# Routed down products: both weight parts in one 512-column matmul, and the two halves added on VectorE

## The reference

```python
out = x @ W_base.T + b_base                       # _L0_cond_ref
lora = einsum('bter,eor,be->bto', einsum('btc,erc->bter', x, As), Bs, w)
h = out + lora * 2.0
scores = softmax(h @ gate_w.T); topk_w, topk_i = top_k(scores, 2)
combine = zeros((T, 8)).at[arange(T)[:, None], topk_i].set(topk_w / topk_w.sum(-1) * 2.5)
g = silu(einsum('td,edf->etf', h, w_gate)) * einsum('td,edf->etf', h, w_up)
y = einsum('te,etd->td', combine, einsum('etf,efd->etd', g, w_down))
return x + y + silu(h @ sw_gate) * (h @ sw_up) @ sw_down
```

## Time and profile before

| | |
|---|---|
| median of 3 runs | 530.56 us (528.44 to 532.13) |
| the profiled execution | 530.44 us |
| its span, first to last instruction | 528.7 us |
| mean granted clock of TensorE | 0.997 of 2.4 GHz |
| busy: PE, DVE, ACT, POOL | 95%, 59%, 52%, 47% of the span |

### The profile page before, as it was taken

One profiled execution on the slowest core, in us unless ns is written; L12 is line 12 of the kernel. 1 busy time (PEld: TensorE's weight loads), 2 busy tenths in 40 slices (PEclk: granted clock), 3 DMA queues, 4 the chain that ended last, 5 costly groups with the idle time before them and its releaser, 6 DMA issues.

```text
span 528.7 us, 10655 instructions
## 1 busy us (share of the span) xinstructions
PE 500.3 (95%) x3284; PEld 461.4 (87%) x3285; DVE 311.4 (59%) x693; ACT 276.3 (52%) x596; POOL 249.4 (47%) x367
## 2 busy tenths in 40 slices
PE   8999998899999999988899999999998999999997
PEld 7988987788888889978899898988988999888886
DVE  2676757998987454434555444444444434368986
ACT  3567776456662445556455455555554645444422
POOL 2142427454650635655876666656666763310100
PEclk9999999999999999999999999999999998999999
DMA  7387479056122253633344334333433442399952
GB/s 221 134 266 202 161 201 323 5 184 180 42 81 40 91 138 91 109 102 91 101 118 110 109 102 117 104 105 100 109 110 100 120 113 66 82 366 311 377 179 79
DMA packets 104923, 74.56 MB, mean 141 GB/s; under 512 B 61930, under 2 KB 99828, under 8 KB 104884
## 3 DMA queue, kind: packets, MB, share of 16 engines
q1 hardware_dynamic: 95764, 55.21, 36.0%
q0 software_dynamic: 6816, 18.62, 11.8%
q10 hardware_dynamic: 2304, 0.26, 0.5%
HBM read 40.25 MB, written 20.32 MB: 115 GB/s over the span
## 4 chain that ended last, share of the span: by engine, by line
PE 57%; DVE 14%; issue 9%; ACT 7%; DMA 5%; SPq 2%; another core or an unknown queue 2%; POOL 1%; DVEq 0%; ACTq 0%; POOLq 0%
PE bank L273 17%; PE bank L275 16%; PE bank L274 16%; PE bank L751 5%; DMA turned<-rows 2%; SPq L342 2%; DVE bank L1213 2%; ACT gt_h L933 1%; ACT x_half L857 1%; DVE acc L1306 1%; DVE xt_l L1028 1%; DMA rows<-x_halves,tok_i 1%; DVE gt_l L1284 1%; PE bank L569 1%
## 5 line engine op out<-in xcount | busy, mean ns | idle before, releaser
L273 PE MATMUL bank<-w_hi,rt_h 128*128 x284 | 98.2, 346 | 0.0
L274 PE MATMUL bank<-w_lo,rt_h 128*128 x284 | 91.9, 324 | 0.0
L275 PE MATMUL bank<-w_hi,rt_l 128*128 x284 | 91.8, 323 | 0.0
L1284 DVE TENSOR_TENSOR gt_l<-bank,gt_h 128x384 fp32r<-128x384 f32 x71 | 39.6, 558 | 84.0 <-ACT gt_h L949 73.5
L544 POOL DMA_INDIRECT y_rows<-y_sb,dst_i x71 | 71.9, 1012 | 11.2 <-POOL spare L458 10.0
L537 POOL DMA_INDIRECT rows<-x_halves,tok_i x71 | 69.5, 979 | 12.5 <-issue 2.2
L933 ACT CAST gt_h<-bank 128x512 fp32r<-128x512 f32 (+1 forms) x48 | 28.1, 586 | 89.3 <-DVE bank L1213 80.5
L273 PE MATMUL bank<-xs_h,sg_h 128*128 128x512 f32 x176 | 70.7, 402 | 0.6 <-ACT act L923 0.4
L273 PE MATMUL bank<-w_hi,gt_h 128*128 (+1 forms) x213 | 61.9, 290 | 9.6 <-DVE gt_l L1284 9.5
L274 PE MATMUL bank<-xs_l,sg_h 128*128 128x512 f32 x176 | 68.9, 391 | 0.0
L275 PE MATMUL bank<-xs_h,sg_l 128*128 128x512 f32 x176 | 68.7, 390 | 0.0
(11 more groups left out here) (181 smaller groups left out, 1228.4 us busy)
## 6 DMA issues: line engine op xcount, KB each, us to landing
pick<-y_rows SPq DMA_DIRECT2D x16, 512.0 KB, 7.9
xin<-in_x_dram SPq DMA_DIRECT2D x8, 512.0 KB, 4.7
x_halves<-x_half SPq DMA_DIRECT2D x8, 512.0 KB, 3.3
w_own<-in_L_ffn_w_gate_dram SPq DMA_DIRECT2D x8, 352.0 KB, 4.3
w_own<-in_L_ffn_w_up_dram SPq DMA_DIRECT2D x8, 352.0 KB, 4.7
y_sb<-in_x_dram SPq DMA_DIRECT2D x5, 512.0 KB, 3.7
base_rows<-y_sb SPq DMA_DIRECT2D x5, 512.0 KB, 2.8
acc<-base_rows SPq DMA_DIRECT2D x5, 512.0 KB, 7.3
```

The source lines that it names most:

```text
L273: pe.matmul(o, lh, rh, start=start, stop=False, skip_group_check=skip)
L274: pe.matmul(o, lh, rl, start=False, stop=False, skip_group_check=skip)
L275: return pe.matmul(o, ll, rh, start=False, stop=stop, skip_group_check=skip)
L1284: v.tensor_tensor(gt_l[i % 2][:, 0:FC * P], TB[:, 0:FC * P], gt_h[i % 2][:, 0:FC * P].bitcast(F32), ALU.subtract).then_inc(s_gl, 1)
```

## The change

The high and the low parts of the routed weights, two tensors before, become the two halves of one tensor, `w_all`. That alone moves nothing, but it lets one matmul read both parts. In `e_down` the first two of the three passes, which had the same stationary operand `gt_h`, become one matmul with 2 x 256 moving columns; it writes high by high into the first half of the bank and high by low into the second half. The third pass stays and adds to the first half. The result of a block is now the sum of the two halves of its bank, and so the copy on ACT is replaced by a `tensor_reduce` with add on DVE, over pairs that lie 256 columns apart. It stands in DVE's loop after `r_word_low` and ahead of `e_low`.

```diff
-        w_hi = sb("w_hi", [P, E, REC], F32R)
-        w_lo = sb("w_lo", [P, E, REC], F32R)
+        w_all = sb("w_all", [P, 2, E, REC], F32R)
...
-                    wh, wl = (w[0:n, bass.ds(e, 1), GU + c * D:GU + (c + 1) * D]
-                              .rearrange("p e d -> p (e d)") for w in (w_hi, w_lo))
-                    mm = three_pass(pe, YE[par][:, 0:D], gt_h[par][0:n, c * P:(c + 1) * P], gt_l[par][0:n, c * P:(c + 1) * P],
-                                    wh, wl, c == 0, c == FC - 1)
+                    cols = slice(c * P, (c + 1) * P)
+
+                    both = w_all[0:n, :, bass.ds(e, 1), GU + c * D:GU + (c + 1) * D].rearrange("p h e d -> p h (e d)")
+                    high = w_all[0:n, 0, bass.ds(e, 1), GU + c * D:GU + (c + 1) * D].rearrange("p e d -> p (e d)")
+                    pe.matmul(YE[par][:, 0:2 * D].rearrange("p (h d) -> p h d", h=2), gt_h[par][0:n, cols], both,
+                              start=(c == 0), stop=False, skip_group_check=True)
+                    mm = pe.matmul(YE[par][:, 0:D], gt_l[par][0:n, cols], high, start=False, stop=(c == FC - 1),
+                                   skip_group_check=True)
...
-            def e_y(i):
-                sc.wait_ge(s_D, UE + i + 1)
-                if i < 4:
-                    sc.wait_ge(s_base, 16 * NPG)
-                else:
-                    sc.wait_ge(s_sc[i % 4], 16 * (i // 4))
-                sc.copy(y_sb[:, i % 4, :], YE[i % 2][:, 0:D]).then_inc(s_y, 1)
...
                 e_silu(i)
-                if i >= 2:
-                    e_y(i - 2)
             e_high(NBLK - 1)
-            e_y(NBLK - 2)
...
                 silu(j, c)
-                if u == UP:
-                    e_y(NBLK - 1)
...
+            def e_y(i):
+                v.wait_ge(s_D, UE + i + 1)
+                if i < 4:
+                    v.wait_ge(s_base, 16 * NPG)
+                else:
+                    v.wait_ge(s_sc[i % 4], 16 * (i // 4))
+                v.tensor_reduce(y_sb[:, i % 4, :], YE[i % 2][:, 0:2 * D].rearrange("p (h d) -> p d h", h=2), AX.X, ALU.add).then_inc(s_y, 1)
...
                     r_word_low(i + 1)
+                if i >= 2:
+                    e_y(i - 2)
                 e_low(i - 1)
...
+            e_y(NBLK - 2)
             e_low(NBLK - 1)
+            e_y(NBLK - 1)
```

More of the change, by code:

```diff
@@ L288, in routed_part @@
             hi = (2 * F, 4 * F, GU + FULL * D, REC)[i]
-            return (w_own[e][0:rows_of, lo:hi], w_hi[0:rows_of, e, lo:hi], w_lo[0:rows_of, e, lo:hi])
+            return (w_own[e][0:rows_of, lo:hi], w_all[0:rows_of, 0, e, lo:hi], w_all[0:rows_of, 1, e, lo:hi])
         N_PART = 4
@@ L759, in e_gate_up @@
                     for k in range(K):
-                        wh, wl = (w[:, bass.ds(e, 1), k * 2 * F + c:k * 2 * F + c + F]
-                                  .rearrange("p e f -> p (e f)") for w in (w_hi, w_lo))
+                        wh, wl = (w_all[:, h, bass.ds(e, 1), k * 2 * F + c:k * 2 * F + c + F]
+                                  .rearrange("p e f -> p (e f)") for h in range(2))
                         mm = three_pass(pe, to[:, 0:F], rt_h[par][:, k * P:(k + 1) * P], rt_l[par][:, k * P:(k + 1) * P],
```

## The result

The changed kernel took 513.24 us (median of 4, 511.38 to 515.79) beside 529.5 us for the kernel before (median of 4, 525.6 to 532.13): a ratio of 0.973, with a 95% interval from 0.967 to 0.978. It is 16 us faster; 4 us were forecast, and the range reached down to 520.5 only.

A forecast was written before the change was run, and what follows sets the result against it. The prediction took PE's instruction list, plus 26 us of stalls in the routed stage, to bound the kernel. From 530.44 us, -2.3 (matmuls), +1.0 (DVE) and -2.7 (feed) gave 526.4, stated as 526.5 us; range 520.5 to 532.5.

The forecast's parts named there:

- What bounds the kernel: PE, busy 95% of the span; routed stage is 233 us of steps at full pace and 26 us of stalls.
- The matmuls, -2.3 us: Down products in the routed stage: merging three pairs of matmuls saves 33 ns a block over 71 blocks.
- the sum: Whole kernel: 530.44 - 2.3 + 1.0 - 2.7 = 526.4 us, given as 526.5 us.
- The work that moves to DVE: Reduction ahead of `gt_l` in DVE's loop: 0.68 us, free in an undisturbed step, +1 us in late ones.
- The +1 us for late steps: DVE's reduction delays steps with late feed or PE signals by 0.05 to 0.2 us each; total between 0 and 2.
- The feed, -2.7 us, between 0 and -5: Copy, scatter, gather, turn: the result leaves `YE` 1.3 us earlier, so turned rows land earlier and PE waits less.
- the last part of the prediction: Profile after: gather 1.3 us earlier, SP's row waits far below 40.6 us, DVE's waits for `turned` below 18.8.
- Smaller late landings elsewhere among the 19 waits may give 1 us more: Part of the feed's gain: DVE's other waits for turned rows, beyond the one long PE wait, 1 us.
- PE's late signals and the stretch at half clock go too: Rival, routed stage: the feed pays more, a fifth of the stalls or more goes, 524 down to 521; chance 0.16.
- the smaller gain of the matmuls: Down products by the skill's gap rule: 8 ns a block, 0.6 us for the kernel, not 2.3.
- the first rival: Feed doesn't pay: late landings are slow transfers or stalls return elsewhere; 529.3 us, or 530.0; chance 0.25.
- the long reduction: Rival: DVE's reduction ahead of `gt_l` delays steps from 1.3 us on; about 534 to 570 us; chance 0.09.

The follow-up runs named there:

- e8: The changed kernel, unedited, run again in a later job: 506.79 us beside 515.65 for the kernel before.
- e11: Kernel before with merged matmuls and ACT's copy moved ahead of `gt_h`, second half of the bank left out: 506.4 us beside 515.65.
- e9: Kernel before with merged matmuls alone, ACT's copy at its old late place, second half of the bank left out: 514.28 us beside 515.65.
- e14: Kernel before, nine matmuls kept, the result copied early by DVE at the reduction's place: 510.92 us beside 516.67.
- e15: Kernel before, nine matmuls kept, ACT's copy moved ahead of `gt_h`: 510.16 us beside 516.67.
- e1: Kernel before with merged matmuls alone, ACT's copy at its old late place, second half of the bank left out: 520.59 us beside 531.4.
- e7: Kernel before with one expert number for twelve blocks, so without a block's loads and address computations on PE: 513.03 us beside 515.34.

## Why the prediction was wrong

- **What bounds the kernel** was right in kind: the routed stage held nearly the whole gain, and the split into list and stalls is the one that explains it.
- **The matmuls, -2.3 us.** The mechanism and the step were right to the hundredth, 3.33 to 3.30 us, and the two far runs cost nothing. At the lower level the merged matmuls returned 1.4 to 4.8 us. At the higher one they returned 10.8 us, since stalls went with them; the sum had no term for that. The gap that the prediction takes from the Trainium skill ("TensorE: Matmul & The Clock Gate", section "Back-to-back issue gap") is called there that of an isolated matmul. The rows are of a stream with a new stationary operand for each matmul, and don't test it; the changed kernel's 0.23 and 0.12 us agree with the rows.
- **The work that moves to DVE.** 0.68 us was forecast and 0.69 measured, at the place forecast. The +1 us for late steps was not seen: with early results, reduction and copy come to the same (e8 and e11).
- **The feed, -2.7 us, between 0 and -5.** The gather came 1.33 us earlier, as forecast, and DVE's listed waits for turned rows fell as the last part of the prediction asked; that SP's would fall too was not borne out by the lists. But the term was mis-sized. "Smaller late landings elsewhere among the 19 waits may give 1 us more" counted only waits that PE itself could be seen to suffer; the runs gave 5.8 and 6.5 us for the early result where no late signals are in play, and nothing for it alone where they are. The 19 waits of the earlier trace rows and the 18 of the earlier trace rows were read as all there were, though more than half of the rises of DMA semaphores weren't recorded; e9, with its copy as late, has 45 and 64.
- **The step that failed** is that the sum left the remaining stalls, 23 of 26 us, as they were. They stood in the prediction as a rival ("PE's late signals and the stretch at half clock go too", 524 down to 521), with a chance of 0.16 and too small still: the changed kernel took 14.9 us from the stalls. Of these 1.3 come from the meeting with GpSimd, which the sum didn't have; some 6 are the feed's by e14 and e15, and the remaining 7 or 8 late signals, which came to 52 us before and 17 after. The split takes prices from one level to the other and is an estimate. The stretch at half clock gave nothing: both profiles have one of 3.4 us in the routed stage.
- **Chances and range.** The bounds of the feed and of the matmuls were drawn from the visible waits alone. 26 us of stalls whose cause was only half known asked for a low end near 515. Two slips of the working changed nothing: with the smaller gain of the matmuls the first rival comes to 531.0, not 530.0, and by its own terms the long reduction decides from 1.35 us, not 1.3.

**Open.** Why PE's signals rise up to 3.9 us late in one job and not in another is not settled, nor why they are fewer in the three kernels with merged matmuls than in the three with nine. Fewer instructions of PE, and the place of the steps against GpSimd's gathers, both fit: in e1 above the gather began at 328.75, between the transposes and the late start. The run that would tell them apart, nine matmuls with the early reduction at the higher level, wasn't had: all four jobs with that kernel fell on the lower one. e7 speaks to the address computations at the lower level alone. And why part of the semaphore records is missing at the higher level is unknown.

## What to carry to other kernels

Take a result out of its bank at the head of the next step when a scatter, a gather and a turn hang behind it: the 1.3 us of slack bought that way was worth 6 us here at one level. At the other it was worth nothing alone, but with merged matmuls, taking the result out at the end of the step cost 12. Divide a stage into steps at full pace and stalls before costing a change, and where the stalls are larger than the edit, let the range reach for them: an edit of 33 ns a block returned 10.8 us. Before a list of waits is read as complete, see whether the records behind it are: the kernel before lists 18 waits of SP for rows, and e7, which differs from it in PE's loads and address computations alone but ran at the lower level, 64 in the same stretch. Compare kernels within one job only, since one kernel's level moved by 3% between jobs, and a gain measured at one level (2.7%) was 1.6 to 2.0% at the other.

## What the runs showed of the hardware

- The same program took 531 us in one job and 515 to 517 in four others, with a granted clock of 0.99 or more throughout. The first and the last job ran on the chip of the same number (2), so the level isn't fixed by that. In the six traces at the higher level 15 to 83 signals of TensorE rose over 0.2 us late (up to 3.9 us), in the fourteen at the lower none; DVE's, ACT's and POOL's never did.
- The six traces at the higher level also hold only 1226 to 1624 rises of DMA semaphores in the routed stage, and the fourteen others 3205 to 3252.
- Two GpSimd subtractions of 128x512 (1.3 us each) held a DVE subtraction of 128x256 with both inputs in SBUF for 2.98 us in place of 0.41, and for 1.34 us where it met only the second. In e14 a copy on DVE (0.3 us elsewhere) took 3.16 us beside them.
- A matmul of 512 columns over two runs of 256, far apart in SBUF, had the next one start after 0.23 us, as contiguous ones do in the earlier trace rows.
- VectorE's sum over pairs, 512 inputs from PSUM to 256 outputs, took 691 ns. The line through the two longer rows (256 inputs in 408 ns, 576 in 730) gives 666 ns, though their outputs were 32 and 72.
